# A decoder layer on one core: where the products of attention and of the FFN stand in PSUM, and in which order each engine comes to them

## The reference

```python
x = x + attn(layernorm(x))            # 16 heads of 16, causal, ALiBi bias, softmax, out @ Wo.T + bo
x = x + xattn(layernorm(x), ctx, mask)# one head of 256: softmax(x @ ctx.T / 16 where mask) @ ctx
x = x + ffn(layernorm(x))             # gelu(x @ q(W_up) + b) @ q(W_down) + b, 256 -> 1024 -> 256
def q(w):                             # MXFP4, blocks of 32 along the rows
    scale = 2 ** (floor(log2(max|w| in block)) - 2)
    return nearest in {0, .5, 1, 1.5, 2, 3, 4, 6} to w / scale, with sign, * scale
```

## Time and profile before

| what | us |
|---|---|
| median of 3 runs | 136.51 |
| lowest and highest run | 135.77, 137.06 |
| the profiled execution, its own time | 137.31 |
| its span, first to last instruction | 135.5 |
| PE busy in the span | 119.1 |
| DVE busy in the span | 108.1 |

### The profile page before, as it was taken

The page is one execution under the profiler, slowest core; times in us unless marked ns, Lnnn a source line. Parts: engine busy times, 40 slices in busy tenths (PEclk is TensorE's granted clock), DMA queues, the critical chain, the costliest instruction groups (busy, mean ns, idle before and its releaser), DMA issues. The chain is left out here.

```text
span 135.5 us, 3237 instructions
## 1 busy us (share of the span) xinstructions
PE 119.1 (88%) x1060; PEld 87.1 (64%) x1060; DVE 108.1 (80%) x253; ACT 84.3 (62%) x180; POOL 75.5 (56%) x140
## 2 busy tenths in 40 slices
PE   0939899999999999979999999764998989999990
PEld 0829346745557785657786766633556878999990
DVE  5382995899998799988989999969977696854632
ACT  2130479349888768856877787757568588545520
POOL 7844400145959833754661667891745979544430
PEclk9995999999999999999999999999599999999999
DMA  4999605999700000000000000000000002020112
GB/s 125 288 356 381 220 6 151 374 344 384 171 0 5 5 0 0 5 0 0 0 7 0 0 5 0 0 0 2 5 0 0 0 0 85 0 77 0 47 35 77
DMA packets 8880, 10.69 MB, mean 79 GB/s; under 512 B 1665, under 2 KB 7937, under 8 KB 8737
## 3 DMA queue, kind: packets, MB, share of 16 engines
q1 hardware_dynamic: 7776, 9.64, 21.2%
q10 hardware_dynamic: 1088, 0.86, 2.1%
HBM read 9.45 MB, written 1.05 MB: 77 GB/s over the span
## 5 line engine op out<-in xcount | busy, mean ns | idle before, releaser
L623 POOL TENSOR_TENSOR s_sb<-s_sb,s_max 128x512 f32<-128x512 f32 x16 | 16.8, 1052 | 24.9 <-DVE s_max L837 24.9
L957 DVE TENSOR_TENSOR h_lo<-h_sb,h_hi 128x256 fp32r<-128x256 f32 x32 | 15.6, 495 | 8.3 <-POOL h_hi L612 8.3
L1132 PE MATMUL bank<-xn_T,w_up_q 128*128 128x256 f16 x128 | 20.1, 291 | 1.4 <-ACT h_sb L753 1.0
L753 ACT ACTIVATE h_sb<-bank,bias_cols 128x256 f32<-128x256 f32 x32 | 14.9, 474 | 9.9 <-PE bank L1132 8.9
L612 POOL CAST h_hi<-h_sb 128x256 fp32r<-128x256 f32 x32 | 14.0, 444 | 11.7 <-ACT h_sb L753 11.7
L1148 PE MATMUL bank<-w_down_q,h_hi 128*128 128x256 f32 x64 | 18.6, 317 | 0.0
L585 POOL TENSOR_TENSOR rstd<-var_eps,minus_half 128x1 f32<-128x1 f32 x24 | 16.0, 666 | 2.0
L1148 PE MATMUL bank<-w_down_q,h_lo 128*128 128x256 f32 x64 | 16.3, 281 | 0.0
L581 POOL TENSOR_SCALAR var_eps<-mean_var 128x1 f32<-128x1 f32 x24 | 8.3, 345 | 14.4 <-DVE mean_var L786 13.6
L653 ACT ACTIVATE xn_T<-bank 128x256 f32<-128x256 f32 x16 | 6.1, 383 | 15.8 <-PE bank L990 15.6
L1003 PE MATMUL bank<-xn_T,w_T 128*128 128x512 f32 x32 | 14.6, 600 | 0.5 <-issue 0.5
(11 more groups left out here) (88 smaller groups left out, 260.8 us busy)
## 6 DMA issues: line engine op xcount, KB each, us to landing
raw_T<-in_W_up_T_dram SPq DMA_DIRECT2D x1, 1024.0 KB, 9.1
raw<-in_W_up_dram SPq DMA_DIRECT2D x1, 1024.0 KB, 11.8
raw_T<-in_W_down_T_dram SPq DMA_DIRECT2D x1, 1024.0 KB, 5.6
raw<-in_W_down_dram SPq DMA_DIRECT2D x1, 1024.0 KB, 8.1
ctx_T<-in_ctx_by_feature_dram SPq DMA_DIRECT2D x1, 1024.0 KB, 10.3
ctx_sb<-in_ctx_dram SPq DMA_DIRECT2D x1, 1024.0 KB, 13.0
out_dram<-x_sb SPq DMA_DIRECT2D x8, 128.0 KB, 1.7
x_sb<-in_x_dram SPq DMA_DIRECT2D x4, 128.0 KB, 3.9
```

Source lines behind the costliest of these rows:

```text
L623: pool.tensor_tensor(tile, tile, s_max[:, u % S_RING, :].unsqueeze(2).broadcast_to([P, HC, S]), ALU.subtract).then_inc(centred, 1)
L753: act.activation(h_sb[:, i % GELU_RING, :], bank[i % 2][:, 0:GN], ACT.Gelu_apprx_tanh, bias=bias_cols[:, BUP + f:BUP + f + 1], scale=1.0 / ...
L957: dve.tensor_tensor(h_lo[:, i % H_RING, :], h_sb[:, i % GELU_RING, :], h_hi[:, i % H_RING, :].bitcast(F32), ALU.subtract).then_inc(split_r ...
L1132: last = pe.matmul(dst[:, 0:GN], w_up_q[:, c, f * P:(f + 1) * P], xn_T16[:, g * GT:(g + 1) * GT, at16:at16 + P], start=(k == 0), stop=(k = ...
```

## The change

- Turned probabilities use bank 2 alone (`PROB_BANKS`); before, banks 2 and 3 by turns.
- The ups of group 0 use bank 7 alone, those of the later groups banks 0 and 1 as before (`UP_BANKS`). The downs use banks 3, 3, 2, 3 by group; before 2, 3, 2, 3.
- Both `pv` of a tile write one bank side by side; `normalise`, `attn_turn` and `attn_copy` are one stage per tile (8), before one per unit (16). `normalise` has one inverse of 128x16 and one product of 128x256 in place of two of 128x8 and two of 128x128; `attn_turn` two transposes, `attn_copy` two copies.
- Moved from DVE to ACT: the first norm of tiles 4 to 7, `v_odd` of half 1 (two copies), and `k_rest` of half 1 (four of the eight masked copies of that half; ACT does all eight). The norms on ACT add a small shift on POOL.
- `WARM` goes from 7 matmuls to 7, 3 and 3, ahead of the first three turns.
- New numbers in the three tables, and new costs of some loads. No transfer is added; SP's order is the same.

```diff
-WARM = 7
+WARM = (7, 3, 3)
...
+
+
+def norm_on_act(n, t):
+    return n != LN1 or t >= HALF
...
+    for i in range(len(WARM)):
+        add("warm", (i,), "pe", 0.22 * WARM[i], [("turn", (LN1, i - 1))] if i else [("load_x", (0,))])
...
+            add("v_odd", (h, pair), "act" if h else "dve", 0.49 if h else 0.6, [("v", (h, pair)), (("v2_zero", "v2_zero2")[h], ())])
...
+        add("prob_T", (u,), "pe", 0.49, [("exp", (u,))], [prob_bank(u)], ("prob_copy", (u,)))
...
+        add("pv", (u,), "pe", 0.59, [("prob_copy", (u,)), ("v_even", (h, 1)), ("v_odd", (h, 1))], [4] if c == 0 else [],
+            ("normalise", (t,)))
...
+        reused = [("attn_turn", (t - 2,))] if t >= 2 else []
+        add("normalise", (t,), "dve", 0.62, [("pv", (EC * t + EC - 1,))] + reused)
+        add("attn_turn", (t,), "pe", 0.25, [("normalise", (t,))], [ATTN_BANK], ("attn_copy", (t,)))
+        add("attn_copy", (t,), "act", 0.54, [("attn_turn", (t,))])
...
-    "attn_turn": 354, "quant": 142, "normalise": 100, "pv": 59, "binade": 55, "prob_T": 49, "x_table": 48,
...
+    "quant": 142, "stats": 131, "amax": 64, "round": 63, "load_qk": 51, "q_exponent": 47, "q_cut": 42,
...
+                if stage == "v_odd" and at[0] == 1:
+                    h, pair = at
+                    act.wait_ge(v2_zeroed[h], 1)
+                    act.wait_ge(v_ready, 2 * h + pair + 1)
+                    act.activation(v2_tiles(h, pair)[S:P, :, :, 1, 0:D], v_tiles(h, pair)[S:P], ACT.Copy).then_inc(
+                        v_odd_ready[1], 1)
...
+                    t, = at
+                    act.wait_ge(attn_turned, t + 1)
+                    for c in range(EC):
+                        last = act.activation(attn_T[:, c, t * P:(t + 1) * P], bank[ATTN_BANK][:, c * P:(c + 1) * P],
+                                              ACT.Identity, bias=bias_cols[:, BV + c:BV + c + 1])
+                    last.then_inc(attn_copied, 1)
...
+                    t, = at
+
+                    dve.wait_ge(pv_ready, EC * (t + 1))
+                    if t >= 2:
+
+                        dve.wait_ge(attn_turned, t - 1)
+                    heads = bank[4][:, 0:H * (D + 1)].rearrange("p (h d) -> p h d", d=D + 1)
+                    step(dve.reciprocal(s_inv[:, t % 2, :], heads[:, :, D]))
+                    dve.tensor_tensor(attn[:, t % 2, :].rearrange("p (h d) -> p h d", d=D), heads[:, :, 0:D],
+                                      s_inv[:, t % 2, :].unsqueeze(2).broadcast_to([P, H, D]),
                                       ALU.mult).then_inc(attn_ready, 1)
...
+                    for i in range(WARM[at[0]]):
...
+                    dst = claim(4, (attn_ready, t + 1)) if c == 0 else bank[4]
...
+                            first = (c * 4 + g) * width
+                            last = pe.matmul(dst[b * S:(b + 1) * S, first:first + width],
...
+                    dst = claim(ATTN_BANK, (attn_copied, t + 1))
+                    for c in range(EC):
+                        last = pe.transpose(dst[:, c * P:(c + 1) * P], attn[:, t % 2, c * P:(c + 1) * P], ident)
+                    last.then_inc(attn_turned, 1)
...
+                    dst = claim(up_bank(i), (gelu_ready, i + 1))
...
+                        claim(down_bank(g), (final_ready, GT * (g + 1)))
...
-K_HEADS = {(0, 0): 2, (0, 1): 2, (1, 0): 2, (1, 1): 2}
+PROB_BANKS = (2,)
+UP_BANKS = ((7,), (0, 1), (0, 1), (0, 1))
+DOWN_BANKS = (3, 3, 2, 3)
+K_HEADS = {(0, 0): 2, (0, 1): 2, (1, 0): 4, (1, 1): 4}
...
+def prob_bank(u):
+    return PROB_BANKS[u % len(PROB_BANKS)]
+
+
+def up_bank(i):
+    banks = UP_BANKS[i // FC]
+    return banks[i % len(banks)]
+
+
+def down_bank(g):
+    return DOWN_BANKS[g]
```

142 lines of the change are left out of this document (60 added, 82 removed).

## The result

| what | before | after |
|---|---|---|
| median of 4 runs each, us | 136.78 | 139.52 |
| lowest and highest run | 135.77, 138.72 | 139.2, 141.03 |
| the profiled execution, its span | 137.31, 135.5 | 139.59, 137.5 |

The changed kernel is slower: ratio 1.025, 95% interval 1.014 to 1.036. I had forecast 132.5, in a range of 128.8 to 137.0. Ratios and intervals leave disturbed runs out, so that a ratio can stand a little off the quotient of two medians. The median rose by 2.7 us: 2.0 is in the span, 0.3 around it, and the profiled execution of before lay 0.5 above its median.

What follows compares the result with a forecast made beforehand. DVE's time up to `w_down_q`, then PE's tail, was taken to set the length: `down 0` minus 8.8, tail plus 4.8, so minus 4.0 us against 136.5, forecast 132.5, range 128.8 to 137.0.

Steps and rivals of the forecast that it cites:

- DVE's stretch: DVE from its first `amax` of W_down to the last `w_down_q` write: 6.6 us less work, write ending at 93.5.
- The start: DVE's first `amax` of W_down, behind the reload: 26.6 in place of 27.14, 0.5 us earlier and not more than 1.0.
- if DVE waits within the stretch as long as before: DVE's idle time up to the `w_down_q` write stays 6.4 us, so the write ends at 95.1.
- the hole: PE's 4.7 us idle between 85.0 and 102.7, ahead of `down 0`; 1.6 of DVE's 2.55 us waiting there taken off.
- DVE idle for over 8 us: Sign that would show the forecast wrong: DVE idle for over 8 us in its stretch.
- 3.0 us off for the keys: Four masked key copies leave DVE, two pairs of 1.76 and 1.43, counted as 3.0 us less in its stretch.
- "slower" rival: ACT's two rows of four masked keys block `exp` and `prob_copy`, losing 6.1 us: 138.6; chance 0.12.
- `down 0` = write + 0.4: On PE, `up 8`, `x_scores 4` and `up 9` put `down 0` 0.4 us behind the `w_down_q` write, at 93.9.
- The chain of gelus: Group 0's ups in one bank take 1.30 us a round; `gelu 0` at 78.5, needed by 83.2, leaves 4.7 in hand.
- The clock: Rival: half clock in bank 7's chain makes rounds 1.75 us, `down 0` at 93.5, 1.7 us lost behind it: 134.2; chance 0.12.
- The tail: PE from `down 0` to its end: 34.6 us in place of 29.8, plus 4.8, from moved stages and a wait.
- the wait at `up 11`: In PE's tail, `up 11` waits for `gelu 9` behind a norm and table load on ACT: 1.6 us idle.

Runs made afterwards that it cites:

- The keys given back: Changed kernel with the masked keys of half 1 divided as before, two of four heads each on ACT and DVE: ratio 1.012 to the kernel before.
- The offload in the order of before: Kernel before with only norms of tiles 4 to 7, `v_odd` and keys of half 1 moved to ACT: 138.2 us, ratio 1.013.
- The filler: Changed kernel with eight unread identity matmuls on PE ahead of the turn of tile 7's second norm: 137.34 us, ratio 1.015 to the kernel before.
- the delayed writes with `low 3` first: Changed kernel, DVE's `w_down_q` writes waiting for POOL's shift of tile 7, and `low 3` ahead of both writes: 136.86 us, ratio 1.013 to the kernel before.
- tile 7 behind: Changed kernel with tile 7's second norm, turn and copy moved behind `down 0` on PE and `gelu 8` on ACT: 136.42 us, ratio 1.002 to the kernel before.
- Delaying the writes alone: Changed kernel with DVE's first `w_down_q` write waiting for POOL's shift of tile 7's second norm, nothing moved: ratio 1.027 to the kernel before.
- two banks: Changed kernel with the ups of group 0 in banks 0 and 1 by turns, not bank 7 alone: ratio 1.028 to the kernel before.
- halves: On top of tile 7 behind, the first four downs wait only for the first half of `w_down_q`, and `down 0` follows `up 7`: ratio 1.019 to the kernel before.
- `x_exp 4` ahead: Changed kernel with two banks for group 0's ups, `x_exp 4` right behind `gelu 7` and `gelu 8` later on ACT: ratio 1.030 to the kernel before.
- the halves and two banks: The kernel with halves, and banks 0 and 1 by turns for the ups of group 0: ratio 1.019 to the kernel before.
- cross attention ahead: On top of tile 7 behind, two banks for group 0's ups and cross attention of tiles 4 and 5 ahead of `down 0`: ratio 1.006 to the kernel before.

## Why the prediction was wrong

**DVE's stretch.** Its work fell by 6.1 us, I had said 6.6; one pair of `normalise` measured 0.26 and 0.42, 0.63 from its start to the start of the next instruction (44.57 to 45.20), as taken. The start came 1.9 us earlier, not 0.5: the reload was issued at 18.96, 1.7 us earlier, where I had said that this hardly moves, and landed in 4.8 us; the first `amax` came 1.5 us behind the landing and did not wait for it. The step that failed is "if DVE waits within the stretch as long as before", with 1.6 us taken off for the hole. Its idle time was 8.75 where I had 4.8, so the stretch is 3.7 us shorter where I had 8.2, and the write ended at 96.7, not 93.5. DVE idle for over 8 us was one of my signs of being wrong. The keys given back show the reason for 3.0 of the 4.5 us by which the stretch is longer than forecast: I had taken 3.0 us off for the keys, but they had stood where PE was full, so their time turned into waiting. The offload in the order of before points the same way for the rest, which no kernel here separates. My "slower" rival had the right objects, the keys, and the wrong effect: ACT's blocks of 2.9 us held PE up by about half a microsecond, not by 6.1 in sum; they bought nothing.

**`down 0` behind the write.** The step "`down 0` = write + 0.4" failed and cost 3.15 us. I had named what PE does between them as `up 8`, `x_scores 4` and `up 9`, and costed their neighbours at nothing. The turn of tile 7, which the change's order puts between `up 7` and `up 8` (the last turn in the second fence on PE), was in none of my terms, though the same order shows it. The filler, the delayed writes with `low 3` first, and tile 7 behind lower the median by 2.2 to 3.1 us (the ratio by 1.0 to 2.2%) and leave DVE's work and the single bank of the ups alone. Only for tile 7 behind does the interval lie clear of the changed kernel's; for the other two the traces carry the argument. The filler divides the loss: about 1.0 of the 3.15 is half clock from the turn to `down 0`, the rest, about 2, the wait itself. The wait had two parents: POOL's slow steps and the place of the turn. With the steps at 0.57 and 0.27 us the norm would have started 1.7 us earlier, an estimate from the rows of both kernels, and most of the wait would be gone, as `low 3` first shows with a wait of 0.30. Delaying the writes alone did not show it, because that edit made `low 3` late.

**The chain of gelus.** The round of one bank was 1.30 us, as worked out. `gelu 0` came at 84.2, not 78.5, and beyond the 83.2 that I had allowed: the last `max` was over at 78.6, where I had said about 75, and 5.6 us lay between, where I had 3.5. Still the bank set nothing while the turn stood where it did, as two banks show.

**The clock.** My rival had half clock inside the chain of the single bank; with the four waits of 0.47 to 0.76 there it stayed full up to 98, and fell behind the wait of 1.99. It cost 1.0 us ahead of `down 0` and 0.6 of the tail. The mechanism was right and its place wrong. The Trainium skill's rule on waits between banks ("TensorE: Matmul & The Clock Gate", section "A second HAM failure mode: psum-queue depth-cycling") put it in that chain: the traces don't bear this out at waits of 0.5 to 0.8 us, and agree that waits between matmuls bring the clock down.

**The tail.** Plus 4.8 forecast, plus 4.3 measured, with the wait at `up 11` of 1.17 where I had 1.6. Of the 4.3, 0.6 is half clock, which I had not counted, so part of the agreement is luck. But the sum hides that this isn't a term to be added to `down 0`: with the halves, an earlier `down 0` lengthened it by 3.8 us.

**In sum,** measured less forecast: start −1.4 (−1.9 for −0.5), stretch +4.5 (−3.7 for −8.2), `down 0` behind the write +3.2, tail −0.5. That is 5.8 of the 6.0 us between −4.0 and +2.0.

## What to carry to other kernels

Before taking work off the busiest engine, look stretch by stretch at what it would do instead; work that stands in another engine's full stretch is free where it is. Walk every engine's new order between the last release and the stage that waits for it, and give each entry its own wait, above all an entry that nobody behind it needs: here a turn on PE and `add_down 5` on POOL. A wait of one to two microseconds on PE is to be priced with the half clock that can follow it, here 1.6 us on top of 2.0.

## What was unexpected on the hardware

- POOL's steps on 128x1 took 1.40 and 1.11 us beside DVE's `w_down_q` writes, 0.57 and 0.27 with DVE idle, the same steps in the same place. The Trainium skill says that GpSimd shares its SBUF interfaces with VectorE and contends with instructions that have two SBUF inputs ("GPSIMD Engine Reference", section "1. Specifications"); these writes have two. This case gives the size: the two steps took 2.5 and 4 times as long. It goes the other way too: a write that began while POOL added a bias (`add_down`, two SBUF inputs as well) took 1.66, 1.70 and 1.64 us in the kernels with delayed writes, with halves and with `x_exp 4` ahead, in place of 1.22.
- After a wait of 1.99 us the granted clock was at or near 0.5 from 98 to 101.6, though PE was busy all of that time; sixteen matmul records, 1.95 us, in the place of the wait kept it at 1.0. Not every such wait does it: with waits of 2.65 and 1.81 us the clock fell before the wait was over, with one of 1.75 about 1.3 us behind it, but with the halves and two banks it was 1.00 for 8.8 us behind a wait of 2.00 that ended at 94.2 and fell only behind 103, after waits of 1.33 and 0.25, and with cross attention ahead it was 1.00 from 85 to 98 through a wait of 2.14 that ended at 89.3. What decides between these is open.
